# Two neighbouring outputs from three products of differences in the first layer of an audio tower

## The reference, cut to what matters

```python
xp = jnp.concatenate([x, pad], axis=-1)
patches = xp[:, :, idx]            # idx: 32 patches, stride 8, length 16
p = transpose(patches).reshape(B, L, V * 16)
h = jax.nn.relu(jnp.einsum('blc,cd->bld', p, W1) + b1)      # 1024 -> 256
out = jnp.einsum('bld,de->ble', h, W2) + b2                 # 256 -> 256
```

## Time and profile before

| | |
|---|---|
| Median of 3 runs | 479.43 us (479.41 to 481.6) |
| Time of the profiled execution | 478.79 us |
| Its span in the profile | 477.1 us |
| Busy: TensorE, VectorE, ScalarE, GpSimd | 417.4, 288.1, 206.8, 170.9 us |
| Matrix products of `layer1` (L1986) | 128 records, 58.7 us busy |
| Mean granted TensorE clock | 0.959 of 2.4 GHz |

### The profile page before, as it was taken

How to read it: one execution, slowest core, us unless ns; L and a number is a source line. 1 busy time by engine, 2 the same in 40 slices (tenths; PEclk the granted TensorE clock), 3 DMA queues, 4 the chain that set the end, 5 groups by cost and what they waited for, 6 DMA issues and landing times.

```text
span 477.1 us, 9442 instructions
## 1 busy us (share of the span) xinstructions
PE 417.4 (87%) x3478; PEld 257.6 (54%) x3490; DVE 288.1 (60%) x886; ACT 206.8 (43%) x380; POOL 170.9 (36%) x141
## 2 busy tenths in 40 slices
PE   2999899998867756787899999999999999999991
PEld 2454555555646645454566666666654545456650
DVE  2788698788789999999974766358630111111110
ACT  3655653655775433255427622444323323323320
POOL 6060000101100076510645355542445554556331
PEclk9999999999879767999999999999999999999996
DMA  8999300100280562740115222332222322223211
GB/s 168 242 203 204 66 21 2 36 14 5 77 321 25 164 218 84 269 157 21 45 23 129 37 45 45 97 63 32 43 45 28 46 49 35 45 44 57 33 23 22
DMA packets 34588, 39.20 MB, mean 82 GB/s; under 512 B 5232, under 2 KB 29040, under 8 KB 34544
## 3 DMA queue, kind: packets, MB, share of 16 engines
q1 hardware_dynamic: 25312, 28.89, 22.6%
q0 software_dynamic: 7040, 9.44, 12.6%
q10 hardware_dynamic: 2192, 0.27, 0.5%
HBM read 27.45 MB, written 8.91 MB: 76 GB/s over the span
## 4 chain that ended last, share of the span: by engine, by line
PE 50%; DVE 18%; DMA 13%; issue 7%; ACT 5%; SPq 5%; POOLq 0%; POOL 0%; DVEq 0%; ACTq 0%
PE psum L2389 20%; PE psum L2410 10%; PE psum L1986 6%; DMA out_dram<-O,dst_i 6%; DMA M3s<-in_x_dram 4%; DMA out_dram<-O,dst_high 3%; PE psum L2399 2%; PE psum L2000 2%; PE psum L2012 2%; DVE st_att L1078 1%; PE psum L2371 1%; SPq L341 1%; DVE H L1328 1%; SPq L354 1%; DVE qtok L1245 1%
## 5 line engine op out<-in xcount | busy, mean ns | idle before, releaser
L1877 DVE TENSOR_TENSOR QT<-QT,psum 128x512 f32<-128x512 f32 x36 | 24.7, 687 | 116.6 <-PE psum L2389 114.3
L2389 PE MATMUL psum<-M1s,KT 128*128 (+2 forms) x176 | 68.9, 601 | 2.2 <-issue 1.8
L2410 PE MATMUL psum<-M3s,KT 128*128 (+1 forms) x352 | 69.3, 383 | 1.5 <-ACT KT L868 0.8
L2389 PE MATMUL psum<-M2s,KT 128*128 (+2 forms) x176 | 67.7, 592 | 0.0
L2410 PEld LDWEIGHTS psum<-M3s,KT 128*128 128x128 f32 (+1 forms) x352 | 50.2, 170 | 24.6 <-issue 16.9
L879 ACT ACTIVATE O<-psum,gate_slot 128x256 f32<-128x256 f32 x36 | 17.1, 475 | 100.4 <-PE psum L2410 91.9
L1986 PE MATMUL psum<-M2s,M1s 128*128 128x512 f32 x128 | 58.7, 602 | 0.7 <-ACT H L686 0.7
L523 POOL DMA_INDIRECT KT<-mixture_rows_in,src_i x36 | 40.5, 1125 | 32.2 <-issue 18.0
L2389 PEld LDWEIGHTS psum<-M2s,KT 128*128 128x128 f32 (+1 forms) x176 | 26.0, 171 | 35.8 <-issue 35.8
L550 POOL DMA_INDIRECT out_dram<-O,src_i x17 | 31.4, 1845 | 34.2 <-ACT O L879 14.5
L864 ACT ACTIVATE QT<-psum 128x512 f32<-128x512 f32 x36 | 21.5, 596 | 40.4 <-PE psum L2389 40.4
(11 more groups left out here) (448 smaller groups left out, 779.2 us busy)
## 6 DMA issues: line engine op xcount, KB each, us to landing
M3s<-in_x_dram SPq DMA_DIRECT2D x4, 1024.0 KB, 13.5
M2s<-in_L_ffn_W_dram SPq DMA_DIRECT2D x1, 4096.0 KB, 15.3
M3s<-in_L_ffn_W_dram SPq DMA_DIRECT2D x1, 4096.0 KB, 17.0
M1s<-in_L_ffn_W_dram SPq DMA_DIRECT2D x1, 4096.0 KB, 14.6
M3s<-in_x_dram SPq DMA_DIRECT2D x3, 992.0 KB, 18.3
M1s<-vtok SPq DMA_DIRECT2D x64, 34.0 KB, 1.9
out_dram<-H SPq DMA_DIRECT2D x4, 512.0 KB, 4.2
M1s<-in_L_tok_W_dram SPq DMA_DIRECT2D x2, 320.0 KB, 9.3
```

The source lines that it names most:

```text
L1877: v.tensor_tensor(sil[:, u, :], sil[:, u, :], bank[3], ALU.mult).then_inc(v_gated, 1)
L2389: last = mm(z[rows, :], xrT[:, u, c, rows], w[:, e, c, :].rearrange("p a h -> p (a h)"), start=(c == 0), stop=(c == CH - 1))
L2410: last = mm(bank[6][rows, 0:DM], actT[:, u, c, rows], M3s[:, e, c, :].rearrange("p a d -> p (a d)"), start=(c == 0), stop=(c == HC - 1))
```

## The change

For two neighbouring outputs the kernel now forms three products, over pairs `l = 2m`, `2m+1`:

`y_2m = W0 (a_2m - a_2m+1) + (W0 + W1') a_2m+1` and `y_2m+1 = W1' (a_2m+2 - a_2m+1) + (W0 + W1') a_2m+1`.

The contraction of one product is 64 channels times 8 samples, in 4 steps of 128 (two samples groups `k` on the partitions, 4 samples `q`), and a product has 256 columns. So `layer1` is 3 kinds (ODD, NEXT, LAST) x 2 halves x 4 = 24 products of 256 columns a step. VectorE computes the differences NEXT and LAST and, once, the sum of the weights `W1sum`; ScalarE copies ODD. ODD's sums go to bank 7 (to banks 0 and 1 in step 0), ScalarE takes them with the bias to `odd_part` (`odd`), VectorE adds them to both outputs of a pair (`hidden_sum`, signal `v_hidden`), and ScalarE takes the relu in place (`hidden`). The second copy of `x` is shifted by 4 samples. `layer1` of step 0 starts with NEXT and LAST and ends with ODD, that of the other steps starts with ODD. The pieces of `layer1` are cut anew, step 0's `layer2` starts without its bias, `ssm_tables` is split between slots 1 and 2, and ScalarE's `hidden`, `exps` and `embed` change places.

```diff
@@ -332,20 +339,20 @@
...
-                sp.dma_start(xin[64:128, i % 2, :, 0:T_IN - STRIDE],
-                             xv[:, SB * i:SB * (i + 1), STRIDE:T_IN]).then_inc(s_x, 16)
+                sp.dma_start(xin[64:128, i % 2, :, 0:T_IN - Q],
+                             xv[:, SB * i:SB * (i + 1), Q:T_IN]).then_inc(s_x, 16)
...
@@ -355,9 +362,8 @@
...
-                sp.wait_ge(a_plane, RH)
-                wait(sp, a_sorted, i - 2)
-                sp.wait_ge(v_plane, (STRIDE - RH) * (i - 1))
+                sp.wait_ge(a_sorted, i - 1)
+                sp.wait_ge(v_plane, 2 * (i - 1))
                 load_x(i)
...
@@ -587,26 +593,23 @@
...
+                for k in range(2):
+                    r = a.activation(xr[64 * k:64 * k + 64, 0, ODD].rearrange("p q (b m) -> p q b m", b=SB),
+                                     xin_m[0:64, 0, 1, Q * k:Q * (k + 1)], ACT.Copy)
+                r.then_inc(a_sorted, 1)
...
-                act.wait_ge(a_pad, i + 1)
+                act.wait_ge(a_pad, i)
                 wait(act, p_layer1, CH * (i - 1))
-                a.activation(xr[:, i % 2, 0:RH], xin_r[:, i % 2, 0:RH], ACT.Copy).then_inc(a_sorted, 1)
+                a.activation(xr[:, i % 2, ODD].rearrange("p q (b m) -> p q b m", b=SB), xin_m[:, i % 2, 1, 0:Q], ACT.Copy
+                             ).then_inc(a_sorted, 1)
...
@@ -687,31 +690,41 @@
...
+                def odd(c):
+
+                    act.wait_ge(p_odd, c + 1 if iA == 0 else CH * (iA + 1))
+                    z = bank[c][:, 0:HALF] if iA == 0 else bank[7][:, HALF * c:HALF * (c + 1)]
+                    a.activation(odd_part[:, c, :], z, ACT.Identity, bias=b1c[:, c:c + 1]).then_inc(a_odd, 1)
+
                 def hidden(c):
-                    act.wait_ge(p_layer1, CH * iA + c + 1)
-                    wait(act, p_layer2, TS * iA)
-                    a.activation(h1T[:, c, :], bank[6 + c], ACT.Relu, bias=b1c[:, c:c + 1]).then_inc(a_hidden, 1)
+                    act.wait_ge(v_hidden, CH * iA + c + 1)
+                    a.activation(h1T[:, c, :], h1T[:, c, :], ACT.Relu).then_inc(a_hidden, 1)
 
                 if iA == 0:
+                    odd(0)
                     hidden(0)
+                    odd(1)
+                    hidden(1)
                     act.wait_ge(v_weight_scale, 1)
                     for w in range(4):
                         r = a.activation(wraw[:, w, :], wraw[:, w, :], ACT.Copy, bias=MAGIC, scale=wmi[:, w:w + 1])
                     r.then_inc(a_weights, 1)
                     act.wait_ge(v_exp, 1)
                     a.activation(sv[:, 4, :], sv[:, 5, :], ACT.Exp, scale=-1.0).then_inc(a_decay, 1)
-                    hidden(1)
+                    embed(0)
                     pad(1)
-                    embed(0)
...
                 elif iA is not None:
+                    for c in range(CH):
+                        odd(c)
                     if iA + 1 < STEPS:
                         pad(iA + 1)
                     if iC is not None and not together:
                         exps(iC, range(0, 2))
-                    hidden(0)
                     if iA + 1 < STEPS:
                         sort_x(iA + 1)
+                    if iC is None:
+                        hidden(0)
...
@@ -743,14 +758,16 @@
...
                 if iA == STEPS - 1:
+                    exps(iC, range(2, BT))
                     hidden(1)
-                    exps(iC, range(2, BT))
...
+                if iA == STEPS - 2:
+                    hidden(0)
...
@@ -943,19 +960,55 @@
...
+            def next_of(out, even, odd):
+
+                v.tensor_tensor(bm(out), even, odd, ALU.subtract).then_inc(v_plane, 1)
+
+            def last_of(out, even, odd, end):
+
+                m = HALF // SB - 1
+                v.tensor_tensor(bm(out)[:, :, :, 0:m], even[:, :, :, 1:], odd[:, :, :, 0:m], ALU.subtract)
+                return v.tensor_tensor(bm(out)[:, :, :, m],
+                                       end.rearrange("p (a b) t -> p a (b t)", a=1).to_broadcast([end.shape[0], Q, SB]),
+                                       odd[:, :, :, m], ALU.subtract)
+
...
+                even, odd = ([xin_m[0:64, 0, e, Q * k:Q * (k + 1)] for k in range(2)] for e in range(2))
+                to = [xr[64 * k:64 * k + 64, 0] for k in range(2)]
+                v.tensor_tensor(bm(to[0][:, NEXT]), even[0], odd[0], ALU.subtract)
+                next_of(to[1][:, NEXT], even[1], odd[1])
+                for k in range(2):
+                    r = last_of(to[k][:, LAST], even[k], odd[k], xin[0:64, 0, :, T_IN - 1:T_IN])
+                r.then_inc(v_plane, 1)
+                dve.wait_ge(d_w1, 32)
+                dve.wait_ge(d_w1_rest, 32)
+                v.tensor_tensor(W1sum, W1s[:, 0:Q], W1s[:, Q:2 * Q], ALU.add).then_inc(v_w1_sum, 1)
+
+            def sort_next(i):
+
+                dve.wait_ge(a_pad, i)
                 wait(dve, p_layer1, CH * (i - 1))
-                for r in range(lo, hi):
-                    v.tensor_copy(xr[:, i % 2, r], xin_r[:, i % 2, r]).then_inc(v_plane, 1)
+                next_of(xr[:, i % 2, NEXT], xin_m[:, i % 2, 0, 0:Q], xin_m[:, i % 2, 1, 0:Q])
+
+            def sort_last(i):
+
+                last_of(xr[:, i % 2, LAST], xin_m[:, i % 2, 0, 0:Q], xin_m[:, i % 2, 1, 0:Q],
+                        xin[:, i % 2, :, T_IN - 1:T_IN]).then_inc(v_plane, 1)
+
+            def hidden_sum(i, c):
+
+                dve.wait_ge(a_odd, CH * i + c + 1)
+                dve.wait_ge(p_layer1, CH * i + c + 1)
+                wait(dve, p_layer2, TS * i)
+                v.tensor_tensor(h1T[:, c, :].rearrange("p (n e) -> p e n", e=2),
+                                bank[6 + c].rearrange("p (e n) -> p e n", e=2),
+                                odd_part[:, c, :].rearrange("p (a n) -> p a n", a=1).to_broadcast([P, 2, HALF]),
+                                ALU.add).then_inc(v_hidden, 1)
...
@@ -1456,21 +1519,27 @@
...
-                if iA is not None and iC is not None and iA + 1 < STEPS:
-                    sort_x(iA + 1, RH, RH + 2)
+                if iA == STEPS - 2:
+                    hidden_sum(iA, 0)
+                    sort_next(iA + 1)
                     turn(iC, 2)
                     turn(iC, 3)
-                    sort_x(iA + 1, RH + 2, STRIDE)
-                elif iA is not None and 0 < iA < STEPS - 1:
-                    sort_x(iA + 1)
+                    hidden_sum(iA, 1)
+                    sort_last(iA + 1)
+                elif iA == 1:
+                    hidden_sum(iA, 0)
+                    sort_next(iA + 1)
+                    hidden_sum(iA, 1)
+                    sort_last(iA + 1)
...
                 if iA == STEPS - 1:
+                    hidden_sum(iA, 1)
                     turn(iC, 2)
                     turn(iC, 3)
...
@@ -1968,32 +2039,70 @@
...
+                for c in range(CH):
+                    for q in range(Q):
+                        mm(bank[6 + c][:, 0:HALF], W1s[:, q, P * c:P * (c + 1)], x[:, NEXT, q, :],
+                           start=(q == 0), stop=(q == Q - 1))
+                pe.wait_ge(d_w1_rest, 32)
...
+            def layer1_first_odd(c):
+
+                pe.wait_ge(a_sorted, 1)
+                pe.wait_ge(v_w1_sum, 1)
+                for q in range(Q):
+                    last = mm(bank[c][:, 0:HALF], W1sum[:, q, P * c:P * (c + 1)], xr[:, 0, ODD, q, :],
+                              start=(q == 0), stop=(q == Q - 1))
+                last.then_inc(p_odd, 1)
...
+            def layer1(i, lo, hi=KINDS * CH * Q):
+
+                if lo == 0:
                     wait(pe, a_embed, i)
-                order = list(range(RH, STRIDE)) + list(range(RH))
-                for n, r in list(enumerate(order))[lo:hi]:
-                    if c == 0 and r >= RH:
-                        pe.wait_ge(v_plane, (STRIDE - RH) * i + r - RH + 1)
-                    elif c == 0 and i == 0:
-                        pe.wait_ge(d_w1_rest, 32)
-                        pe.wait_ge(a_plane, r + 1)
-                    elif c == 0 and r == 0:
-                        pe.wait_ge(a_sorted, i)
-                    last = mm(bank[6 + c], W1s[:, r, P * c:P * (c + 1)],
-                              xr[:, i % 2, r].rearrange("p b l -> p (b l)"),
-                              start=(n == 0), stop=(n == STRIDE - 1))
-                if hi == STRIDE:
-                    last.then_inc(p_layer1, 1)
+                    pe.wait_ge(a_sorted, i + 1)
+                for n in range(lo, hi):
+                    c, q = n // Q % CH, n % Q
+                    if n < CH * Q:
+                        last = mm(bank[7][:, HALF * c:HALF * (c + 1)], W1sum[:, q, P * c:P * (c + 1)],
+                                  xr[:, i % 2, ODD, q, :], start=(q == 0), stop=(q == Q - 1))
+                        if q == Q - 1:
+                            last.then_inc(p_odd, 1)
+                        continue
+                    c, e = divmod(n // Q - CH, 2)
+                    if q == 0 and c == 0:
```

(50 more changed lines are left out.)

94 lines of the change are left out of this document (53 added, 41 removed).

## The result

The changed kernel takes **485.14 us** in the median of 4 runs (483.95 to 486.45), the kernel before 479.42 us (479.33 to 481.6) beside it. The ratio on record is 1.0087, with a 95% interval of 1.0059 to 1.0116; the quotient of the two medians would be 1.0119. By either it is slower; the median lies outside the range given, the ratio on record, times 479.42, would be 483.6, at its end. The profiled execution took 485.64 us, its span is 483.9 us (before 477.1). A hole is a wait of TensorE, and "the clock" is its granted clock, 1.00 at 2.4 GHz and 0.50 at 1.2.

A forecast was written before the change was run, and what follows sets the result against it. TensorE was taken as the bound from 12 to 117 us, VectorE from 117 to 236. Step and slot terms summed to 0.5 us less of a 13.9 us ceiling, giving 478.9 us, range 475.5 to 483.8.

The forecast's parts named there:

- What a product costs: TensorE's layer1: products of 256 columns take 0.435 us against 0.87 for 512; four steps give 13.9 us less, the ceiling.
- What VectorE and ScalarE get: Work before 117 us: VectorE some 4 us more, a difference 1.22 us; ScalarE's ODD copy 2.0 us.
- the differences read slowly: Rival, VectorE's differences: two strided operands could double their time, adding 3 to 5 us, 482 to 484; chance 0.10.
- Step 0: nothing is won: First step: layer1 ends earlier, but TensorE waits for v_ternary and begins step 1 at 32.9, 0.9 us late.
- the walk: The prediction's tracing of starts and waits through steps 0 and 1 and slots 2 and 3; rounding half a us.
- Step 1: one us is won: Second step: x of step 2 on ScalarE sets qkv's start, 46.0 instead of 47.04; gain 1.0 us.
- Slots 2 and 3: VectorE takes the gain back in part; the projection starts at 103.85 after 3.8 us idle, later stages 0.5 us early.
- The clock falls: Rival: TensorE drops to 1.2 GHz in the hole before att_proj, 3.6 to 7.5 us more, 482.5 to 486.4; chance 0.25.
- The chances: Weights on outcomes: forecast 0.50, clock 0.25, slow differences 0.10, VectorE's gaps 0.15; same 0.54, slower 0.30, faster 0.16.
- Ceiling and sum: Whole kernel: at most 13.9 us of TensorE could be saved, of which 0.5 us was to reach the end.

The follow-up runs named there:

- e1: Changed kernel with the differences of steps 1 to 3 reading contiguous weights instead of x: 483.57 us, ratio 1.0051.
- e17: Changed kernel with samples kept in pairs, so VectorE and ScalarE read runs of 8 bytes and TensorE reads at a stride of 8 bytes: 483.61 us, ratio 1.0056.
- e8: Changed kernel with other operands and strides for the six differences of steps 1 to 3, values not kept: differences take 1.2 or 1.9 to 2.0 us.
- e10: Changed kernel with the state tables made whole in slot 1, as in the kernel before: 486.63 us, ratio 1.0110.
- e18: Changed kernel with samples kept in pairs and nine wide float32 fillers (products nobody reads) in TensorE's four holes: 479.81 us, ratio 0.9984.
- e5: Changed kernel with contiguous reads for the differences of steps 1 to 3 and 63 fillers in TensorE's four holes: 482.74 us, ratio 1.0026.
- e19_pairs_fill_turns: e18 with slot 2's last two turns ahead of the hidden sums and differences, and one filler there instead of three: 479.27 us, ratio 0.9968.
- e7: Changed kernel with three moves of order on ScalarE and VectorE, and 48 fillers in TensorE's holes: 484.16 us, ratio 1.0053.
- e9: Changed kernel with planes kept with q innermost, so TensorE reads one q at a stride of 16 bytes: 519.18 us, ratio 1.0788.
- e6: Changed kernel with three moves of order on ScalarE and VectorE, without fillers: 486.47 us, ratio 1.0102.
- e4: Changed kernel with VectorE's differences and ScalarE's copy of ODD walked with q innermost, planes unchanged, writes scattered: 485.54 us, ratio 1.0107.
- e14: Changed kernel with 63 fillers in TensorE's four holes and the second difference of steps 1 to 3 on GpSimd: 493.12 us, ratio 1.0246.

## Why the prediction was wrong

- **"What a product costs" was right**: eight products of 256 columns take 3.69 us, and TensorE lost 10.8 us of busy time before 117 us in spite of four falls of the clock.
- **"What VectorE and ScalarE get" is the step that failed, in one term**: the difference, 1.22 us taken, 1.88 measured, and with contiguous operands 1.215 (e1). By rows the new work of VectorE is 26.4 us for 14.6 taken off, 11.8 us more where the forecast had 4; the windows show 5.6 because what stood at their end slid past 117 us. The rival "the differences read slowly" had it, with 0.10. It was argued away by rows that did not bear on it: L1120 reads without a stride, and L958 (1.22 ns an element at a stride of 32 bytes) was never set beside a contiguous copy. The same trace has a contiguous instruction with one operand, L1016, 1293 ns for 2048 elements, 0.63 ns each, so that "one strided operand costs nothing" was not shown. ScalarE's row was the one of the right kind, and stood there.
- **"Step 0: nothing is won"** is where the first of it landed: step 1 began at 35.93 instead of 32.9. VectorE's preparation ended at 18.3 us instead of 15.3, but the DMA hid most of that: the sum of the weights began at 18.66, 0.7 us late. TensorE itself started at 13.22 (12.17 in the walk) and ended `layer1` at 24.6 (22.8), and the hole of 2.00 us ahead of `layer2`, where it waits for ScalarE, was not in the walk; e17 has one of 1.95 with fast reads. Behind it the clock fell. In e8, with the same work and no fall, step 1 begins at 34.83: 1.1 of the 3.0 us are the clock's.
- **"Step 1: one us is won"**: ScalarE's `pad` came at 42.64 instead of 41.94, but x did not bind. `in_columns` did, at 47.41, and `qkv` came at 49.37 instead of 46.0. In e10, without the fall behind the hole of 2.0 us, `qkv` came at 48.78.
- **"Slots 2 and 3"**: the hole ahead of the projection is there as forecast, 3.39 us and released by VectorE's sum; only the clock in it was not. With fast reads it is as long: 3.38 in e1, 3.18 in e17. The hole ahead of `values` of slot 2 was in the walk too (69.6 to 73.4), but not among the places where the clock might fall; it came at 77.8. The tables came out as the walk had them, near nothing (0.7 us, e10_tables).
- **"The clock falls"** had 0.25, one hole and a doubtful second, and the sum put it at nothing: that is the second term that failed. In the profiled execution there were four falls. Its price, 3.6 to 7.5 us, holds the 3.5 us of e18 against e17 at its lower end.
- **The chances** took the two as ways to 484 or 486.4, and the range's end of 483.8 had no case with both. They came together, and the runs show them as separate costs that about add up (e5). The holes do not come from the slow reads in the main: with contiguous ones e1 has holes of 2.00, 3.57 and 3.38 us and a fall behind each.
- **Ceiling and sum**: that only a trace of the 13.9 us can reach the end was right. With both costs removed the time is not told from the kernel before (e18, 0.9963 to 1.0006); 1.5 us are won only with slot 2's turns first as well (e19_pairs_fill_turns).

**Open.** What the wait of "issue" is that came with 63 fillers; no run moved it alone. What each of the four falls costs was tried in no pair of kernels of its own; the profiles give 1.1 us for that of step 0 (e8) and some 0.5 for that of step 1 (e10, `qkv` 48.78 against 49.37), and the other two are not priced apart. Why the clock held with 63 fillers in most kernels and with 9, and fell once with 48 (e7), is open too, and so is what slot 3 would do if the x of step 2 landed earlier.

## What to carry to other kernels

Before work is moved from a bound engine to one that has room, price the new instruction by a row with the same operands, access pattern included; with none, take both prices to the end of the sum. Choose a layout with all its readers in view: here two neighbouring elements served VectorE, ScalarE and TensorE alike, while four were free for two of them and doubled the third. And when a busy TensorE gets less to do, the holes are not free: here they cost clock in what came behind them, and the end was set by waits that TensorE's own work had covered before.

## What was not expected of the hardware

- A float32 instruction of VectorE with two operands takes 1.19 ns an element if all three streams give two neighbours or a stride of 8 bytes, and 1.87 to 2.0 if one of them, the write too, has a stride of 32 bytes or more (e8). ScalarE's copy of 1024 elements goes from 1.05 us (e9) to 1.95 (the kernel after).
- TensorE reads a float32 moving operand at a stride of 8 bytes 2 to 3% slower than at none (387 ns a record against 379, e17), and at 16 bytes at half the speed: 7.40 us for eight products in place of 3.69 (e9).
- The same hole of 2.00 us ahead of `layer2` of step 0 brought the clock down in the profiled executions of the kernel after, e1 and e10 (0.84 from 21 to 32 us), and not in those of e6 and e8 (1.00), with the same work up to there. The hole of 2.0 us ahead of step 1's ODD products did so in the kernel after and e4 (16 records of ODD in 5.38 us in the kernel after), and not in e1 and e10 (16 records in 3.69 in e10).
- GpSimd takes 3.8 ns an element for the strided difference, twice VectorE's 1.88, and while it runs a VectorE instruction of 4 elements took 3.4 to 3.6 us instead of 0.16, three times of three (e14).
